# Layer 0 rebuilt: modulation as columns on ScalarE, gates made once, and each batch's projections moved into the attention slots of the batch before it

## What is computed

```python
mod = (silu(c) @ wmod).reshape(4, 6, 1, -1)
sa, ca, ga, sb, cb, gb = (mod[:, i] for i in range(6))
ga = (2 * (ga >= 0) - 1) * maximum(abs(ga), 0.25)      # gb likewise
h = layernorm(x) * (1 + ca) + sa
x = x + ga * attention(h)
h = layernorm(x) * (1 + cb) + sb
x = x + gb * ffn(h)
```

## Time and profile before

| | |
|---|---|
| time, median of 3 runs | 1458.23 us (1455.41 to 1460.9) |
| the profiled execution's own time | 1461.47 us |
| its span, first to last instruction | 1459.7 us |
| PE busy | 1270.8 us (87%) |
| DVE busy | 1043.7 us (71%) |
| ACT busy | 678.6 us (46%) |
| POOL busy | 542.2 us (37%) |
| mean granted TensorE clock | 0.933 of 2.4 GHz |

### The profile page before, as it was taken

How to read it: one execution, slowest core, us unless ns; L and a number is a source line. 1 busy time by engine, 2 the same in 40 slices (tenths; PEclk the granted TensorE clock), 3 DMA queues, 4 the chain that set the end, 5 groups by cost and what they waited for, 6 DMA issues and landing times.

```text
span 1459.7 us, 25278 instructions
## 1 busy us (share of the span) xinstructions
PE 1270.8 (87%) x7740; PEld 956.4 (66%) x7740; DVE 1043.7 (71%) x3041; ACT 678.6 (46%) x1605; POOL 542.2 (37%) x496
## 2 busy tenths in 40 slices
PE   5898887776844899999899999999999899996998
PEld 3553443344443677777677778777788688785887
DVE  5766768777657876877876877876777766674773
ACT  2334534343403645545645545645655645652332
POOL 0000000000000988889888889888721300000000
PEclk8898989888856999999999999999999999998999
DMA  5121100101111010210110210110200200000000
GB/s 167 43 66 35 32 23 27 44 20 37 40 48 62 30 39 11 96 38 0 39 39 10 95 36 4 33 36 8 91 32 19 70 29 7 22 0 0 15 14 29
DMA packets 29850, 54.31 MB, mean 37 GB/s; under 512 B 5664, under 2 KB 21872, under 8 KB 29280
## 3 DMA queue, kind: packets, MB, share of 16 engines
q1 hardware_dynamic: 26544, 42.93, 8.9%
q0 software_dynamic: 2096, 6.51, 1.4%
q10 hardware_dynamic: 1152, 4.19, 0.7%
HBM read 41.86 MB, written 11.63 MB: 37 GB/s over the span
## 4 chain that ended last, share of the span: by engine, by line
PE 53%; DVE 34%; issue 10%; ACT 3%; DVEq 0%; DMA 0%; ACTq 0%; SPq 0%
PE bank L1307 10%; PE bank L1285 7%; PE bank L263 6%; PE bank L264 6%; PE bank L265 6%; DVE qkst L977 4%; DVE negmax L912 4%; PE bank L1296 4%; DVE qk L996 4%; PE bank L1074 3%; PE bank L1275 3%; PE bank L1204 2%; PE bank L1189 2%; PE bank L332 2%; DVE negmax L1009 1%
## 5 line engine op out<-in xcount | busy, mean ns | idle before, releaser
L528 POOL TENSOR_SCALAR gtmp<-gidx,lut 128x344 f32<-128x344 int32 (+2 forms) x210 | 301.5, 1436 | 21.3
L531 POOL TENSOR_TENSOR gacc<-gacc,gtmp 128x344 f32<-128x344 f32 (+2 forms) x210 | 183.4, 873 | 17.5
L1285 PE MATMUL bank<-kT,qT 128*128 128x128 f32 (+3 forms) x512 | 179.8, 442 | 9.2 <-ACT probs L720 9.1
L521 POOL DMA_DIRECT2D gidx<-in_idx_gate x4 | 2.2, 543 | 465.3 <-DMA h_saved<-wft 465.3
L1307 PE MATMUL bank<-pT,v 128*128 128x128 f32 x1280 | 155.4, 277 | 12.2 <-ACT pT L713 12.2
L912 DVE TENSOR_REDUCE negmax<-bank 128x1 f32<-128x512 f32 (+3 forms) x176 | 109.8, 639 | 74.3 <-PE bank L1206 73.3
L1009 DVE TENSOR_REDUCE negmax<-bank 128x1 f32<-128x128 f32 (+3 forms) x256 | 123.4, 484 | 54.6 <-PE bank L1286 53.4
L720 ACT ACTIVATE probs<-bank,negmax 128x128 f32<-128x128 f32 (+3 forms) x256 | 135.6, 530 | 49.9 <-DVE negmax L1009 47.3
L1307 PEld LDWEIGHTS bank<-pT,v 128*128 128x128 f32 x1280 | 148.0, 192 | 15.9 <-DVE oL L1019 15.9
L977 DVE BATCH_NORM_STATS2 qkst<-qk 128x6 f32<-128x128 f32 x512 | 110.0, 279 | 63.4 <-issue 63.4
L263 PE MATMUL bank<-wgH,hL 128*128 128x512 f32 x384 | 153.6, 400 | 0.1
(11 more groups left out here) (191 smaller groups left out, 2809.0 us busy)
## 6 DMA issues: line engine op xcount, KB each, us to landing
hH<-h_saved SPq DMA_DIRECT2D x16, 512.0 KB, 4.0
hL<-h_saved SPq DMA_DIRECT2D x16, 512.0 KB, 4.7
qst<-q_parts SPq DMA_DIRECT2D x96, 64.0 KB, 2.3
wg<-in_wqkv SPq DMA_DIRECT2D x4, 1536.0 KB, 8.3
wo<-in_wo SPq DMA_DIRECT2D x4, 512.0 KB, 9.2
out<-x SPq DMA_DIRECT2D x8, 256.0 KB, 2.1
x<-in_x SPq DMA_DIRECT2D x1, 1536.0 KB, 10.0
wmod<-in_wmod SPq DMA_DIRECT2D x1, 1536.0 KB, 11.9
```

The lines of the kernel that those rows point to most:

```text
L528: link(pool.tensor_scalar(tmp if j else acc, part, float(j), lut1[0:rows, j:j + 1], ALU.is_equal, ALU.mult))
L531: link(pool.tensor_tensor(acc, acc, tmp, ALU.add))
L1285: pe.matmul(bank[SCORE_BANKS[i % 3]][:, 0:n], qT[:, h, t * P:n], kT[:, h, 0:n], start=True, stop=False)
```

## The change

- **Modulation as columns.** Shift and scale of all four norms are made as columns (features on partitions, one column for each batch) by small matmuls (`columns`) and kept in modc. A norm on DVE ends after the statistics and the Newton steps, with one product more (minus mean times reciprocal root). ACT then makes the normalized x from it (`act_scale`, four instructions), PE transposes it, ACT applies 1 + c and s as scale and bias on the transposed tile (`act_mod`, to hf) and then copies the high part from hf (`act_high`); DVE takes the rest from hf (`dve_low`).
- **Gates once.** The gates of both layers are made once, for all batches, on four rows of a tile (grows, gffn), stored to DRAM by POOL and loaded back repeated over the partitions. The factor GB is multiplied into the scale and shift that the router's token path uses (GC0, GS0), and into the expert bias (ebg), so the step L880 becomes a step on hN earlier in the chain (n = 20 and 21).
- **Projections in the slots.** Batch 0 is projected at the start. Batch b + 1 is projected by `pre0` inside the 44 slots of batch b, with tiles of its own (q32, khi, kmi, klo, hH2, hL2, norm_a0's hA and hFA). The statistics of batches 1 to 3 are made in one go before the first slot. SP's list interleaves storing and loading of q with the maxima.
- **Maxima by DVE.** After the two splits DVE transposes the maxima in blocks of 32 x 32; SP writes them with four DMAs of 64-byte runs. PE and ACT have no part in it. TURN is 16.
- **Other.** Scores use 3 banks; a score waits for the maximum of three units before. `after0` has 49 steps with other distances. The order of the first loads differs. The loops of layer 1's `swiglu` are written out. The DVE carriers (L381) in the norms of these stages are gone.

```diff
+TURN = 16
+S_BANKS = (0, 1, 4)
 VALUE = TURN + 2
-AFTER = VALUE + 3
+PRE = SLOTS0
+AFTER = SLOTS0 + VALUE + 1
+CHAIN = 49
...
+            def dve(self, dve, ch, b, tiles=QT, at=0):
...
+            def act_scale(self, act, b, ready, at=0):
+                act.wait_ge(self.st, ready)
+                for i in range(QT):
+                    last = act.activation(self.xn[:, i, :], x[:, b * QT + i, :], ACT.Identity,
+                                          bias=self.small[:, 3, at + i:at + i + 1],
+                                          scale=self.small[:, 2, at + i:at + i + 1])
+                last.then_inc(self.h, 1)
...
+            def act_mod(self, act, b):
+                for k in range(KT):
+                    act.wait_ge(self.tp, b * KT + k + 1)
+                    act.activation(self.hf[:, k, :], bank[6 + k][:, :], ACT.Identity,
+                                   bias=modc[:, 1, self.which, k, b:b + 1],
+                                   scale=modc[:, 0, self.which, k, b:b + 1]).then_inc(self.hm, 1)
+            def act_high(self, act, b, high):
+                for k in range(KT):
+                    act.wait_ge(self.hm, b * KT + k + 1)
+                    act.activation(high[:, k, :], self.hf[:, k, :], ACT.Copy).then_inc(self.hi, 1)
...
+            def dve_low(self, dve, b, high, low):
+                for k in range(KT):
+                    dve.wait_ge(self.hi, b * KT + k + 1)
+                    dve.tensor_tensor(low[:, k, :], self.hf[:, k, :], f32(high[:, k, :]), ALU.subtract).then_inc(self.lo, 1)
...
             def load_negmax(b, g):
...
-                sp.wait_ge(nm_copied, b * NG + g + 1)
-                for j in range(NMP):
-                    sp.dma_start(qst[SHIFT + j:SHIFT + j + 1, g * HG * SEQ:(g + 1) * HG * SEQ].rearrange(
-                        "p (i q) -> p i q", q=P), nmt[j * ITEMS:(j + 1) * ITEMS, :]).then_inc(nm_ready, 16)
...
+                sp.wait_ge(nm_turned, b * NG + g + 1)
+                rows = qst[SHIFT:ROWS0, g * HG * SEQ:(g + 1) * HG * SEQ].rearrange("p (i j q) -> p i j q", j=QT, q=VW)
+                for j in range(QT):
+                    sp.dma_start(rows[:, :, j, :], nmt[j * VW:(j + 1) * VW, :]).then_inc(nm_ready, 16)
...
+            for b in range(NB):
+                if b:
+                    load_negmax(b - 1, NG - 1)
+                    load_q(b, 2)
                 load_negmax(b, 0)
-                reload_q(b, 3)
+                if b:
+                    load_q(b, 3)
+                if b + 1 < NB:
+                    store_q(b + 1)
                 load_negmax(b, 1)
-            load_negmax(NB - 1, 2)
-            load_negmax(NB - 1, 3)
+                if b + 1 < NB:
+                    load_q(b + 1, 0)
+                load_negmax(b, 2)
+                if b + 1 < NB:
+                    load_q(b + 1, 1)
+            load_negmax(NB - 1, NG - 1)
...
+            pool.wait_ge(gates_saved, 6 * 16)
+            pool.dma_start(gb64[:, :, :].rearrange("p b d -> p (b d)"),
+                           gates[GB0].to_broadcast([NE, NB * D])).then_inc(gates_loaded, 16)
+            pool.dma_start(ebg[NE:NE + 1, :, :].rearrange("p b d -> p (b d)"), gates[GS0]).then_inc(gates_loaded, 16)
+            for tile, i, kind in ((gate0, 0, GA0), (gate0, 1, GC0), (gate1, 0, GA1), (gate1, 1, GB1)):
+                pool.dma_start(tile[:, i, :, :].rearrange("p b d -> p (b d)"),
+                               gates[kind].to_broadcast([P, NB * D])).then_inc(gates_loaded, 16)
+            pool.wait_ge(gates_loaded, 6 * 16)
...
+            def pre0(n, b):
+                if n == 2:
+                    if b:
+                        norm_a0.wait_ready(act, b - 1)
+                    else:
+                        act.wait_ge(cols_ready, 2)
+                    norm_a0.act_mod(act, b)
+                elif n == 3:
+                    act.wait_ge(qkv_pe, b * (KT + 2))
+                    norm_a0.act_high(act, b, hH2)
...
-                elif n == 2:
+            norm_a0.dve(dve, ch, 1, (NB - 1) * QT, QT)
+            dve.wait_ge(rows_pe, 2)
+            raw = bank[5][:, 0:D]
+            ch.step(dve.tensor_scalar(gsign[:, :], raw, 0.0, 2.0, ALU.is_ge, ALU.mult))
+            ch.step(dve.tensor_scalar(gsign[:, :], gsign[:, :], -1.0, None, ALU.add))
+            ch.step(dve.tensor_tensor(gmag[:, :], raw, gsign[:, :], ALU.mult))
+            dve.scalar_tensor_tensor(out=grows[:, :], in0=gmag[:, :], scalar=0.25, in1=gsign[:, :], op0=ALU.max,
+                                     op1=ALU.mult).then_inc(rows_ready, 1)
+            dve.wait_ge(rows_ready, 1)
+            gb = grows[VW:2 * VW, :]
+            dve.scalar_tensor_tensor(out=gffn[VW:2 * VW, 0:D], in0=bank[3][VW:2 * VW, D:2 * D], scalar=1.0, in1=gb,
+                                     op0=ALU.add, op1=ALU.mult).then_inc(rows_ready, 1)
+            dve.tensor_tensor(gffn[VW:2 * VW, D:2 * D], bank[3][VW:2 * VW, 0:D], gb, ALU.mult).then_inc(rows_ready, 1)
...
+            def after0(n, b):
+                ch = ch_after
+                last = b == NB - 1
+                if n == 4:
                     for k in range(KT):
                         dve.wait_ge(ot_hi, b * KT + k + 1)
                         dve.tensor_tensor(oL0[:, k, :], bank[6 + k][:, :], f32(oH0[:, k, :]), ALU.subtract).then_inc(ot_lo, 1)
-                elif n in (4, 5):
-                    t2 = n - 4
+                elif n in (8, 9):
+                    t2 = n - 8
+                    dve.wait_ge(gates_loaded, 6 * 16)
                     dve.wait_ge(y0_pe, b * 2 + t2 + 1)
                     ch.step(dve.tensor_tensor(ytmp[:, :, :], bank[6 + t2][:, :].rearrange("p (t d) -> p t d", d=D),
-                                              modb(0, b, GA).to_broadcast([P, 2, D]), ALU.mult))
+                                              gate(gate0, 0, b).to_broadcast([P, 2, D]), ALU.mult))
                     ch.step(dve.tensor_tensor(xb(b, 2 * t2, 2), xb(b, 2 * t2, 2), ytmp[:, :, :], ALU.add))
-                elif n in NORM_AT[6]:
-                    for part in NORM_AT[6][n]:
-                        norm_f0.dve_part(part, dve, ch, b, b)
-                elif n == 17:
-                    norm_f0.dve_part(NORM_PARTS - 1, dve, ch, b, b)
+                elif n in (10, 11, 12, 13):
+                    for part in (2 * (n - 10), 2 * (n - 10) + 1):
+                        norm_f0.dve_part(part, dve, ch, b)
                 elif n == 19:
+                    norm_f0.dve_low(dve, b, hH, hL)
...
+                elif n == 24:
...
                     ch.step(dve.tensor_tensor(lg[:, :, :], bank[6][:, 0:QT * NE].rearrange("p (t e) -> p t e", e=NE),
                                               rbias[:, :].rearrange("p (one e) -> p one e", one=1).to_broadcast([P, QT, NE]), ALU.add))
                     dve.tensor_reduce(rsm[:, 0, :], lg[:, :, :], AX.X, ALU.max, negate=True).then_inc(r_nmax, 1)
-                elif n == 22:
+                elif n == 27:
                     dve.wait_ge(r_exp, (b + 1) * QT)
...
-                        dve.tensor_tensor(nmp[:, 1, :], nm, nmp[:, 0, :], ALU.subtract).then_inc(nm_split, 1)
-                    i, batch = at_step(n, VALUE + 2, b, scores, values)
-                    if i is not None and i % GU == GU - 1:
+                        dve.wait_ge(max0, b * SLOTS0 + (g + 1) * GU)
+                        ch_nm.step(dve.tensor_copy(nmp[:, 0, :], nm))
+                        ch_nm.step(dve.tensor_tensor(nmp[:, 1, :], nm, nmp[:, 0, :], ALU.subtract))
+                        if b * NG + g:
+                            dve.wait_ge(nm_ready, (b * NG + g) * QT * 16)
+                        dve.transpose(nmt[:, :], nmp[:, :, :].rearrange("p j i -> p (j i)")).then_inc(nm_turned, 1)
...
+            def columns(first, last):
+                for kind in range(2):
+                    for i in range(first, last):
+                        l, *cs = NORM_MODS[i]
+                        c = cs[kind]
+                        for m in range(KT):
+                            for k in range(KT):
+                                mm = pe.matmul(cols[:, kind, i, m, :], wmod[:, l, k, c * D + m * P:c * D + (m + 1) * P],
+                                               sc[:, l, k, 0:NB], start=(k == 0), stop=(k == KT - 1))
+                mm.then_inc(cols_pe, 1)
+            pe.wait_ge(consts, 8)
...
+            def pre0(n, b):
+                if n == 1:
+                    if b:
+                        pe.wait_ge(k_low, b)
+                        pe.wait_ge(v_read, b)
+                    if b >= 3:
+                        pe.wait_ge(r_nmax, b - 2)
+                    norm_a0.pe(pe, b)
+                elif n in (12, 13):
+                    m = n - 12
+                    norm_a0.wait_ready(pe, b)
+                    if b >= 3:
+                        pe.wait_ge(r_read, b - 2)
+                    if b == 0:
+                        pe.wait_ge(w0_lo, 1)
+                    w = slice(m * P, (m + 1) * P)
```

(7 more changed lines are left out.)

830 lines of the change are left out of this document (388 added, 442 removed).

## The result

The changed kernel takes 1389.28 us (median of four runs, 1389.01 to 1391.75) against 1459.04: a ratio of 0.9529, interval 0.9506 to 0.9551. Forecast were 1361 us and a range of 1336 to 1400. The direction and the range hold, the size is 28 us short. One run of version e1 took 6579.63 us and is left out of what is said of e1. The profiled execution spans 1387.2 us.

The account below looks back on a forecast made before the run. Modulation products bound the start, PE and DVE waiting on each other the slots, a serial chain the end. Savings of 66.7 + 17 + 11.5 + 2 = 97 from 1459.7 gave a span of 1363, median 1361 us, range 1336 to 1400.

Parts of the forecast that it names:

- Start: Stage before the first maximum: 110.7 us becomes 44, since only batch 0 is projected there; saving 66.7, bounds 41 and 53.
- Work in the slots: Engine work in the four batches' slots: in batch 2 PE goes from 61.7 to 68.3 us, DVE from 61.7 to 58.5.
- I keep 3.7 of 20: Batch 2's slots: of 20 us PE idle time only 3.7 stays, giving 72 us; all slots 270.2 to 253, saving 17.
- third bank: Scores in the slots: a third bank lets PE run two units ahead, removing its 6.5 us wait for maxima in batch 2.
- the slots keep their stalls: Rival, 15%: all idle time in the slots stays, so they take 291 us and the kernel 1399.
- PE waits for DMA of the maxima: Sign of a wrong prediction; the DMA in the slots was priced at 4.8 us against 5 slots, 5.3 to 8 us.
- PE isn't held: Rival, 14%: without stalls PE's clock stays at 2.4 GHz, the slots take 232 us and the kernel 1340.
- Projections in the slots: Each of batches 1 to 3 projected inside the slots: 6.84 us of PE products plus eight transposes.
- the start is partly given back in the slots: Rival, 4%: projections, splits and copies run one after the other in the slots, 12.7 us more for each of three; 1399.
- End: End stage of layer 0, a serial chain: 81.8 us becomes 70, saving 11.5, bounds 4 and 17.
- a norm less heavy makes 22: End stage: the last attention output's transposes start 22 us after the last maximum instead of 26, a saving of 4.
- Layer 1: Layer 1 and its feed-forward part: only the first norm_f1's lighter apply is exposed; with a written-out loop it saves 2 us.

Follow-up runs that it names:

- e1: Changed kernel with the scaling of norm_f0 and norm_a1 inside the slots done by DVE instead of ACT; 1381.65 us.
- e4: Changed kernel with modulations, projections and splits of batches 1 to 3 run ahead of the slots again; 1407.26 us.
- e3: Changed kernel with two score banks instead of three and the attention output turned into bank 4 instead of shared bank 5; 1393.42 us, ratio 0.9531.
- e6: Changed kernel with products that nothing reads (18, 12 and 20) added on PE in the waits of the end stage; 1388.77 us.
- e9: e2 with products that nothing reads added on PE, 17 a batch in the slots of batches 1 to 3 and 28, 12, 42 in the end stage; ratio 0.9467.
- e7: e2 with steps 2 to 25 of the chain behind the attention one slot later on all engines; ratio 0.9475.
- e10: e2 with norm_f0's transpositions and what follows up to the routing's maxima two slots later, and the next norm_a0 too; ratio 0.9482.
- e11: e2 with DVE's split of the next batch's q moved from steps 14 and 15 to 26 and 27, q stored later; ratio 0.9450.
- e5: Changed kernel with the edits of e1 and e2 both at once; 1376.48 us.
- e2: Changed kernel with the turned scores one slot later (TURN 17), the batch's chain keeping its place; 1378.73 us.
- e12: Changed kernel with TURN 17, e11's late q split, e9's added products in the end stage only, and DVE scaling for the last batch only; 1371.17 us.

## Why the prediction was right, and where it was 28 us short

**Start: right, with some luck.** 42.8 against 44. PE was done with v at 27.3, not at about 30, and its column and row products took 13.0 us, not 11; the two errors nearly cancel. The first maximum follows the six gate steps on DVE, 40.27 to 42.72, 2.45 us where 2.7 were forecast (chain of the changed kernel):

```profile
40.27 0.44 DVE gsign L868
...
42.39 0.33 DVE gffn L877
42.76 2.95 DVE negmax L964 x5
```

**Work in the slots: right in sum, in part by luck.** The forecast's PE work a batch (42.8, 61.9, 68.3, 60.8) makes 233.8 us; measured are 45.8, 62.8, 66.5 and 58.1, 233.2 in sum. The errors of the batches cancel, and so do two terms: three projections took 28.9 us of PE's work (e4) where 23.5 were priced, and the rest 204.2 where some 210 were. DVE's 58.5 in batch 2 came out at 58.9. ACT's 43 of batch 2 came out at 41.4.

**Idle time in the slots: this step failed.** "I keep 3.7 of 20", and 5, 4 and 6 in the other batches, 18.7 us in all; measured are 6.8, 6.9, 12.0 and 12.7, 38.4 us. So 17.0 of the 55.4 us of before went, where 36.7 were to go. The working took the waits for split maxima (5.7), for maxima (6.5) and for rests (3.7), asked for each whether the change removes its cause, found that it does, and took their sum off the time. The causes were removed, and the third bank and the longer distances did cut their waits. But e3 shows that 20 us of a wait can be put back (with 6.5 of another taken away) without batches 1 to 3 growing, and e1 that 4.7 us can be taken from one without batches 1 and 2 shrinking. I read it so: PE, DVE and ACT each go through one list in slot order and hand to each other several times a slot; the wait named by the trace is merely where PE stands when the others are late. Here two more conditions spoke in the profile and I priced neither. The projections fill PE for 12 us at a stretch while DVE gathers late work. And PE would have had to be busy for 95% of batch 2 with DVE at 81% in a chain of dependent steps: no stage of the earlier trace rows has PE above 89%, and that was the batch with the least in it. With the 233.8 us of work and that best idle share, 11%, the slots would have come to 263 us, with the 24% of batches 2 and 3 to 308; measured are 14%. The rival "the slots keep their stalls" named what happened, in a form too strong (291; the measured idle time lies halfway between it and the forecast), and at 15% it was too cheap.

What does bound batches 1 to 3 isn't settled. It isn't one wait (e1, e3), hardly the clock (e6, e9), not the place of the chain or of the q split in their slots (e7, e10, e11). It is in part work: without projections batches 0 to 2 are 7.7, 9.8 and 6.1 us shorter (e4), and 1.3 and 2.5 us more of DVE lengthened batches 1 and 2 by 1.4 and 2.1 (e5, but not e1). That it is the handing over between three lists that are each full for stretches is argued from these runs, not shown.

**The DMA of the maxima: a condition that failed, mildly.** "PE waits for DMA of the maxima" stood among the signs of a wrong prediction, and it does, for 7.2 us. The price was 0.7 + 2.3 + 1.8 = 4.8 us against 5 slots of 1.05 us in batch 0. Issue and landing are what was priced, 0.61 (forecast 0.58) and 1.69 (1.8); here by line and in the chain, and then a wait in batch 0 (SP's four issues, and PE's first product that needs them):

```profile
L457 SPq DMA_DIRECT2D qst<-nmt x64: 598/611/832, 51.8 to 317.7; - x64
...
317.69 1.69 DMA qst<-nmt
...
69.70 2.57 SPq L457 DMA_DIRECT2D qst<-nmt  x4
...
73.41 0.61 PE L1239 MATMUL bank<-qst,kst 98*128 98x512 bf16 x1 [2.02 <-DMA qst<-nmt]
```

So each term was right. What failed is the other side, five slots of mean length: DVE ended the group's last maximum at 69.1 and SP issued as soon as the transposition was done, but PE, which runs ahead of the maxima, stood at the product from 71.4 on, 2.3 us after the maximum, and started it 4.3 us after it. With one slot more (e2) the wait is gone. The rule of the Trainium skill, "DMA: Bandwidth & Descriptors" (Specifications), that pieces should have at least 512 B, shows nowhere here: with pieces of 64 bytes in place of 256 the landing is no longer than in the earlier trace rows.

**The banks and PE's clock.** The third bank was credited with the 6.5 us of batch 2; e3, which undoes it together with the shared bank 5, found 3.6 us at most, in batch 0 alone. The rival "PE isn't held" had the full clock shorten the slots; e9 had nearly the full clock there, and they were no shorter, with 15.2 us of added products in them.

**Projections in the slots: right.** 7.8 us each, as priced (e4); PE's work for them is dearer, 9.6, but lies in part in its waits. The rival "the start is partly given back in the slots" (12.7 each on top) is refuted.

**ACT.** Scaling a tile costs 0.585 us, more than the 0.4 that I estimated from copies; with the scaling off ACT (e1) batches 1 and 2 took the same time. No table is loaded between exponentials: one load ahead of the first SiLU and one ahead of the exponentials of layer 0 stand in the first 400 us (the first row has min, median and max in ns; the other two busy us, mean ns and idle time before).

```profile
L326 ACT ACTIVATE hN<-x,sm x48: 583/585/600, 147.4 to 1345.8; 128x256 f32<-128x256 f32 x48
...
L609 ACT ACT_TABLE_LOAD x1 | 1.3, 1283 | 3.2 <-POOL vS L529 3.2
L727 ACT ACT_TABLE_LOAD x1 | 1.3, 1283 | 0.0
```

That agrees with the Trainium skill, "ScalarE: Activation LUTs" (Table sets), which lists identity in every set.

**End: 6 us short.** Of the saving of 11.5, 5.8 came. The largest term that failed is "a norm less heavy makes 22": oTok's transpositions of the last batch start at

```profile
341.06 1.95 PE bank L1185 x8
```

26.7 us behind the last maximum, as the 26 of before. Ahead of them stands norm_a1 of batch 2, with its scaling on ACT and its two modulations of 0.78 us each. From there to layer 1 it takes 49.3 us against 55.4 before (the earlier trace rows for its beginning), 6.1 less where 7.5 were forecast. e1 puts the price of ACT's scaling in this stage at 2.5 us, e9 that of the low clock at 4.7; together they are less than the sum (e12).

**Layer 1.** 0.2 us instead of 2; with 991 to 1001 us for the same code in thirteen profiles, nothing can be said of it.

## What to carry to other kernels

In a stage where several engines work through lists in a common order, sum up each engine's work, which comes out well, and don't take a wait off the time because its cause goes: first ask what share of idle time the best comparable stage has, and claim no more than that. A wait's length in the trace isn't its price; the cheapest way to the price is to put the wait back, or double it, and see whether the stage grows. In the serial end stage single savings did shorten the stage, that of the clock by 4.7 us, but there too two of them together gave less than their sum.

## What the runs showed of the hardware

- ACT's Identity with a scale and a bias for each partition took 0.585 us for 128 x 256 in fp32 (x64), 0.18 us more than VectorE's tensor_scalar for the same (0.408 us, e1).
- DVE turned 32 x 32 blocks of a bf16 tile of 128 x 32 in 0.211 us.
- Products that nothing reads, 128 x 512 in bf16, have 0.377 us each in the trace of fast stretches, but overlap: 24 of them stand in 5 us, one every 0.21 us (e9):

```profile
345.00:350.00 5.00, 5.00 (x24) 2.15 (x22) 4.49 (x22) 0.00 (x0) 0.00 (x0) 1.00 0.01 2
```

- They kept the granted clock up: in the end stage it went from 0.64 to 0.83, and the four transpositions on the path from 1.13 to 0.67 us. In e6, where the products ended 4.3 us before the wait did, the transpositions behind them ran at the low level again.
